# Decay exponents of a state-space layer: from a TensorE product to a broadcast load and sums on GpSimd

## What is computed

```python
xBC  = causal_depthwise_conv(W_in @ layernorm(u))       # four taps
cum  = cumsum(-softplus(A_log), within the chunk)
diff = cum[..., :, None] - cum[..., None, :]            # (q, k)
decay = exp(where(k <= q, diff, -inf))
y_intra = einsum('bchqk,bckhp->bcqhp', (C @ B^T) * decay, x)
states  = einsum('bckhn,bckhp->bchpn', B * exp(cum[-1] - cum), x)
y_inter = einsum('bcqhn,bchpn->bcqhp', C * exp(cum), previous state)
out = (y + D * x) * silu(z + z_bias) @ W_out
```

## Time and profile before

| | |
|---|---|
| median of 3 runs (lowest, highest) | 406.16 us (405.43, 406.35) |
| the profiled execution: its time, its span | 406.83 us, 405.1 us |
| TensorE busy | 386.7 us (95%) |
| VectorE busy | 332.6 us (82%) |
| ScalarE busy | 226.6 us (56%) |
| GpSimd busy | 176.2 us (43%) |
| moved by DMA | 21.13 MB, mean 52 GB/s |
| share of the chain of waits: TensorE, VectorE, ScalarE, GpSimd | 70%, 13%, 8%, 2% |

### The profile page before, as it was taken

The page is one execution under the profiler, slowest core; times in us unless marked ns, Lnnn a source line. Parts: engine busy times, 40 slices in busy tenths (PEclk is TensorE's granted clock), DMA queues, the critical chain, the costliest instruction groups (busy, mean ns, idle before and its releaser), DMA issues.

```text
span 405.1 us, 8904 instructions
## 1 busy us (share of the span) xinstructions
PE 386.7 (95%) x3023; PEld 299.3 (74%) x3023; DVE 332.6 (82%) x564; ACT 226.6 (56%) x422; POOL 176.2 (43%) x208
## 2 busy tenths in 40 slices
PE   8998999999999999996989999899999999999996
PEld 8686676766766767764767777568888888888886
DVE  5988899999999999997989938738958759696685
ACT  6766556465565564568676632664554545546541
POOL 3699411101111101106456920235686665867661
PEclk9999999999999999999999999989999999999999
DMA  6311220322220122213411150000102020200003
GB/s 186 100 54 25 58 64 8 115 56 61 62 59 28 41 59 63 61 35 109 128 49 25 49 162 1 0 2 1 60 19 78 3 78 13 65 0 2 0 2 104
DMA packets 35932, 21.13 MB, mean 52 GB/s; under 512 B 17048, under 2 KB 33760, under 8 KB 35904
## 3 DMA queue, kind: packets, MB, share of 16 engines
q1 hardware_dynamic: 35904, 20.78, 18.3%
HBM read 18.13 MB, written 1.31 MB: 48 GB/s over the span
## 4 chain that ended last, share of the span: by engine, by line
PE 70%; DVE 13%; ACT 8%; issue 6%; POOL 2%; ACTq 0%; DVEq 0%; POOLq 0%
PE bank L1283 22%; PE bank L1259 10%; PE bank L1249 9%; PE bank L1478 8%; PE bank L1252 5%; PE bank L1398 3%; PE bank L1269 2%; PE bank L1466 2%; DVE conv L1228 2%; PE bank L1307 2%; PE bank L1425 2%; DVE conv L1021 2%; POOL el L656 1%; ACT conv L695 1%; PE bank L1486 1%
## 5 line engine op out<-in xcount | busy, mean ns | idle before, releaser
L1021 DVE SCALAR_TENSOR_TENSOR conv<-bank,taps,conv 128x510 f32<-128x510 f32 (+2 forms) x204 | 149.8, 745 | 17.4 <-ACT conv L695 12.3
L1283 PE MATMUL bank<-uth,parts 128*128 128x512 f32 x272 | 95.3, 407 | 1.1 <-DVE utl L1004 0.9
L695 ACT ACTIVATE conv<-bank,tap_b,taps 128x512 f32<-128x512 f32 x68 | 52.9, 777 | 69.6 <-PE bank L1283 58.9
L569 POOL TENSOR_TENSOR ce<-conv,ecx 128x512 f32<-128x512 f32 x15 | 19.4, 1291 | 117.5 <-DVE conv L1021 117.5
L1283 PEld LDWEIGHTS bank<-uth,parts 128*128 128x128 f32 x272 | 51.0, 187 | 18.9 <-issue 3.5
L651 POOL TENSOR_TENSOR ul<-conv,uh 128x512 fp32r<-128x512 f32 x32 | 42.9, 1357 | 40.5 <-ACT uh L922 27.5
L656 POOL TENSOR_TENSOR el<-conv,parts 128x512 fp32r<-128x512 f32 x30 | 44.3, 1504 | 30.3 <-ACT parts L934 30.3
L1283 PE MATMUL bank<-utl,parts 128*128 128x512 f32 x136 | 53.5, 393 | 0.0
L1216 DVE CAST uh<-conv 128x512 fp32r<-128x512 f32 x28 | 26.0, 966 | 22.5 <-ACT conv L918 21.9
L1228 DVE TENSOR_TENSOR conv<-conv 128x512 f32<-128x512 f32 x32 | 31.4, 1014 | 11.9 <-ACT conv L939 11.8
L1106 DVE SCALAR_TENSOR_TENSOR g<-dec,bank 128x512 f32<-128x512 f32 x64 | 40.8, 678 | 0.0
(11 more groups left out here) (208 smaller groups left out, 743.3 us busy)
## 6 DMA issues: line engine op xcount, KB each, us to landing
w_raw<-in_L_attn_W_in_dram SPq DMA_DIRECT2D x17, 256.0 KB, 3.2
ecx<-ecum_dram SPq DMA_DIRECT2D x32, 128.0 KB, 2.9
ew_raw<-in_L_ffn_Wup_dram SPq DMA_DIRECT2D x7, 256.0 KB, 2.9
ew_raw<-in_L_ffn_Wgate_dram SPq DMA_DIRECT2D x7, 256.0 KB, 3.1
ew_raw<-in_L_ffn_Wdown_dram SPq DMA_DIRECT2D x7, 256.0 KB, 3.8
xres<-in_x_dram SPq DMA_DIRECT2D x2, 512.0 KB, 4.2
out_dram<-xres SPq DMA_DIRECT2D x4, 256.0 KB, 2.1
yi<-yev SPq DMA_DIRECT2D x56, 16.0 KB, 1.8
```

The costliest lines, as they stand in the source:

```text
L695: act.activation(conv[q][:, j, HALF * h:HALF * (h + 1)], bank[u % 2][:], ACT.Identity, bias=tap_b[q][:, j:j + 1], scale=taps[q][:, j, TAPS ...
L1021: dve.scalar_tensor_tensor(out=dst[:, :, d:SEQ], in0=src[:, :, 0:SEQ - d], scalar=taps[q][:, j, TAPS - 1 - d:TAPS - d], in1=dst[:, :, d:SE ...
L1283: ins = pe.matmul(bank[u % 2][:], w, x_t, start=(i == 0), stop=(i == 3 * KD - 1))
```

## The change

The exponents are no longer a matmul. `load_cumb` brings, for each unit, the four rows of cumulative sums broadcast to all 128 partitions (256 KB) into its own tile `cumb[u]`; GpSimd overwrites what the mask excludes with -1e30 (`mask`, an affine select in place) and adds the negative sum of each key (`spans`), and ScalarE takes the exponential of that tile into one of four `dec`. The masks and adds of units 0 and 1 are made a body ahead, those of 2 and 3 in the pair's own body. Each load waits for the exponential of the same unit of the pair before. `turn_w` takes the place of exponents 0 and 1; the state is turned into bank 4. The taps of two units are interleaved (`crossed_taps`), and what waits for them counts by `taps_by`. The extra work of ScalarE and GpSimd is moved to earlier bodies, and the unrolled part begins at pair 8.

```diff
-            def load_cum(m, q):
...
+            def load_cumb(m, u):
+
+                h, j = u // 2, u % 2
+                at_least(sp, exp_done, 4 * (m - 2) + u + 1)
+                row = T * (2 * (m - 1) + j) + T // 2 * h
+                sp.dma_start(cumb[u][:], cum_dram[row:row + T // 2, :].partition_broadcast(P)).then_inc(cumb_in[u], 16)
...
+        def taps_by(m, u):
+
+            in_turn = isinstance(m, int) and m < 2
+            return 12 * m + ((3, 6, 9, 12) if in_turn else (4, 6, 10, 12))[u]
...
-            for n in range(PAIRS - 4, PAIRS + 1):
+            for n in range(PAIRS - 8, PAIRS + 1):
...
-                if n == PAIRS - 3:
+                if n == PAIRS - 5:
                     load_expert(0, 0)
-                if n == PAIRS - 2:
+                if n == PAIRS - 4:
                     load_expert(1, 1)
...
                 if n < PAIRS:
-                    load_cum(n + 1, 1 - q)
+                    load_cumb(n + 1, 0)
+                    load_cumb(n + 1, 1)
                 if 1 < n < PAIRS:
                     sp.wait_ge(y_read, n - 1)
                     place_y(n - 1, 1 - q, yev_out[1 - q])
                 if n < PAIRS:
                     load_ecx(n + 1, 1 - q)
+                    load_cumb(n + 1, 2)
                 if n + 3 <= PAIRS:
                     load_w(n + 3, 1 - q)
                 if n + 2 <= PAIRS:
                     load_taps(n + 2, q)
+                if n < PAIRS:
+                    load_cumb(n + 1, 3)
...
+            def mask(u):
+
+                pool.affine_select(out=cumb[u][:], in_=cumb[u][:], compare_op=ALU.is_ge, fill=NEG, base=0,
+                                   pattern=[[0, T // 2], [1, P]], channel_multiplier=-1).then_inc(masked, 1)
+
+            def spans(n, q, u):
+
+                pool.wait_ge(masked, 4 * (n - 1) + u + 1)
+                h, j = u // 2, u % 2
+                from_s = ncp[q][:, j, 2 * h:2 * h + 2, :].rearrange("p b c -> p (b c)").unsqueeze(2).to_broadcast([P, T // 2, P])
+                pool.tensor_tensor(cumb[u][:], cumb[u][:], from_s, ALU.add).then_inc(span_done, 1)
...
+            pool.wait_ge(ncum_done, 1)
+            copy_ncum(1, 1)
...
+            mask(0)
+            mask(1)
+            spans(1, 1, 0)
+            spans(1, 1, 1)
...
             def body(n, k, q):
                 end = isinstance(n, int) and n == PAIRS
+                pool.wait_ge(cumb_in[2], 16 * n)
+                pool.wait_ge(cumb_in[3], 16 * n)
                 if end:
+                    mask(2)
+                    mask(3)
+                    spans(n, q, 2)
+                    spans(n, q, 3)
                     decay_c_half(n, q, 0)
                     decay_c_half(n, q, 1)
...
+                    gate_late()
+                    rest_weights(1, 1, 1)
+                    rest_weights(1, 1, 2)
+                    return
+                at_least(pool, stT_done, n - 1)
+                copy_xs(n + 1, 1 - q)
+                mask(2)
+                mask(3)
+                spans(n, q, 2)
+                spans(n, q, 3)
+                at_least(pool, y_done, 4 * (n - 1))
+                copy_x(n + 1, 1 - q)
+                decay_c(n, k, q)
+                at_least(pool, exp_done, 4 * (n - 1))
+                pool.wait_ge(cumb_in[0], 16 * n + 16)
+                pool.wait_ge(cumb_in[1], 16 * n + 16)
+                copy_ncum(n + 1, 1 - q)
+                mask(0)
+                mask(1)
+                pool.wait_ge(ncp_done, n + 1)
+                spans(n + 1, 1 - q, 0)
+                spans(n + 1, 1 - q, 1)
...
+                if n == 1:
+                    weigh_context()
+                if n in (PAIRS - 7, PAIRS - 6):
...
+                if n in (PAIRS - 5, PAIRS - 4):
+                    pool.wait_ge(z_gated, 4)
+                    gate_y(0, n - PAIRS + 5)
+                if n == PAIRS - 3:
...
+                    rest_weights(0, 0, 0)
+                if n == PAIRS - 2:
+                    rest_weights(0, 0, 1)
+                    rest_weights(0, 0, 2)
+                    rest_weights(1, 1, 0)
+                if n == PAIRS - 1:
+                    gate_y(1, 0)
+                    gate_y(1, 1)
...
-            act.copy(cr[1][0][STEPS:ROWS, :, :, :], rows_wide()).then_inc(cr1_done, 1)
...
+            act.activation(ncum[:].rearrange("p c r -> p (c r)"), bank[7][:, P:3 * P], ACT.Identity, scale=-1.0).then_inc(ncum_done, 1)
...
-                act.activation(dec[b][:], bank[4 + b][:], ACT.Exp).then_inc(exp_done, 1)
+                a = 4 * (n - 1) + u
+                act.wait_ge(span_done, 4 * (n - 1) + u + 1)
+                at_least(act, g_done, a - 3)
+                act.activation(dec[u][:], cumb[u][:].rearrange("p i t -> p (i t)"), ACT.Exp).then_inc(exp_done, 1)
...
-                if isinstance(n, int) and n == PAIRS - 4:
-                    gate_of_z(u)
-                if isinstance(n, int) and n == PAIRS - 3:
-                    pairwise(u)
-                if isinstance(n, int) and n >= PAIRS - 2 and u < 3:
+                if isinstance(n, int) and n in (PAIRS - 8, PAIRS - 7) and u % 2:
+                    gate_of_z(2 * (n - PAIRS + 8) + u // 2)
+                if isinstance(n, int) and n in (PAIRS - 6, PAIRS - 5) and u % 2:
+                    pairwise(2 * (n - PAIRS + 6) + u // 2)
+                if isinstance(n, int) and n in (PAIRS - 3, PAIRS - 2) and u < 3:
...
+            def crossed_taps(m, q, v):
+
+                done = 12 * m + 3 * v
+                for i, (u, d) in enumerate(((v, 1), (v, 2), (v + 1, 1), (v, 3), (v + 1, 2), (v + 1, 3))):
...
+                    if d == 1:
+                        dve.wait_ge(acc_first, 4 * m + u + 1)
+                    else:
+                        dve.wait_ge(tap_done, done + (0, 1, 0, 2, 3, 5)[i])
...
-                        other_taps(n, q, 3)
+                        if isinstance(n, int) and n == 1:
+                            other_taps(n, q, 3)
...
-                        other_taps(n + 1, 1 - q, 0)
-                        other_taps(n + 1, 1 - q, 1)
+                        crossed_taps(n + 1, 1 - q, 0)
...
-                        other_taps(n + 1, 1 - q, 2)
+                        crossed_taps(n + 1, 1 - q, 2)
...
-                pe.wait_ge(tap_done, 12 * n + (9, 12)[h])
+                pe.wait_ge(tap_done, taps_by(n, 2 + h))
...
-                exponents(n, k, q, 2)
-                exponents(n, k, q, 3)
                 b_dot_c(n, q, 1)
...
                 turn_state(n - 1)
                 weigh(n - 1, 1 - q, 2)
-                exponents(n, k, q, 0)
-                exponents(n, k, q, 1)
+                if not last(n, 2):
+                    turn_w(n + 2, k + 1, q, lambda: None)
                 from_state(n - 1, 0)
```

More of the change, by code:

```diff
@@ L103, in decoder_layer @@
         cum = sb("cum", [P, 2 * P])
[L104 to L105 removed]
+        ncum = sb("ncum", [P, 2, P])
+        ncp = [sb(f"ncp{i}", [P, 2, NSEQ, 2]) for i in range(2)]
         ecum = sb("ecum", [P, P])
@@ L204, in decoder_layer @@
         taps_in = [sem(f"taps_in{i}") for i in range(2)]
-        cum_in = [sem(f"cum_in{i}") for i in range(2)]
+        cumb_in = [sem(f"cumb_in{u}") for u in range(4)]
         ew_in = [sem(f"ew_in{i}") for i in range(2)]
@@ L372, in _ @@
                              ecum[NH * b:NH * (b + 1), :]).then_inc(ecum_out, 16)
-            sp.wait_ge(const_done, 3)
-            sp.wait_ge(cr1_done, 2)
             sp.wait_ge(cum_out, 16 * NSEQ)
-            load_cum(1, 1)
+            for u in range(4):
+                load_cumb(1, u)
             sp.wait_ge(ecum_out, 16 * NSEQ)
@@ L612, in body @@
+                mask(0)
[3 more added lines that the diff above has]
+                spans(n + 1, 1 - q, 1)
+                if not isinstance(n, int):
+                    return
+                if n == 1:
+                    weigh_context()
+                if n in (PAIRS - 7, PAIRS - 6):
+                    for v in range(2 * (n - PAIRS + 7), 2 * (n - PAIRS + 7) + 2):
                         pool.wait_ge(zgate_done, v + 1)
@@ L621, in body @@
-                    if isinstance(n, int) and n == PAIRS - 2 and u == 3:
-                        for j in range(3):
-                            rest_weights(0, 0, j)
-                    if isinstance(n, int) and n == PAIRS - 1 and u == 2:
-                        rest_weights(1, 1, 0)
-                        rest_weights(1, 1, 1)
-                        gate_y(1, 0)
-                        gate_y(1, 1)
-                        rest_weights(1, 1, 2)
-                    if u == 1 and end:
-                        gate_late()
@@ L870, in body @@
                 copy_state_turned(n)
+                if not first:
+                    act.wait_ge(ce_done, n - 1)
                 beside(n, m, km, r, 2)
@@ L1279, in project_pass @@
                         pe.wait_ge(utl_done, 2 * u + 2)
-                    at_least(pe, tap_done, 3 * (4 * m + u - 1))
+                    if u >= 2:
```

(3 more changed lines are left out.)

169 lines of the change are left out of this document (50 added, 119 removed).

## The result

The changed kernel takes 415.59 us, median of 4 runs (415.15 to 417.32), the kernel before 406.19 beside it (405.43 to 406.35): a ratio of 1.0226, 95% interval 1.0183 to 1.027. The forecast, 409.8, had the direction and not the size, and 415.59 lies above the range. The profiled execution took 415.15 with a span of 413.2.

A forecast was written before the change was run, and what follows sets the result against it. TensorE was taken to bound a pair at 12.47 us, VectorE right behind. Start +1.6, bodies 3 to 7 -1.6, bodies 8 to 15 -1.1, end +4.2 and clock +0.5 gave +3.6: 409.8 us, range 401.5 to 414.5.

The forecast's parts named there:

- the forecast loop: Plain pair: fourth tap 2.83, signal 0.1, b_dot_c to the next block's first tap 3.70, block 4.2, two g 1.30: 12.13 us.
- start: Before S(3): GpSimd's masks and adds, exponentials and split_w delay the first crossed block; +1.6 us, bounds 0.8 to 2.5.
- bodies 8 to 12: ScalarE's table load, gates of z and sigmoids, moved to these bodies, hold back copies; 4.4 us over plain pairs.
- the end's mechanism: Last pair: late loads and GpSimd's queue delay ce, so TensorE's state product starts 4.2 us later; lower bound 1.2.
- Loads: Plain pairs: 256 KB loads land after 3.2 us, worst 5.1; slack 1.8, so landing may take 5; no stall.
- rival 4: GpSimd bounds, masks at 1.29: near 421 us, chance 0.04; aside, loads landing after 5.5 us: 412 to 415, chance 0.04.
- at most about 0.4 us a pair: Plain pairs: most that removing TensorE work alone can bring, as VectorE has 12.07 us of work and 0.42 idle.
- at no cost there: Plain pairs: turn_w moves into TensorE's wait for ScalarE's copy of the state, priced at nothing.
- split_router: Bodies 8 to 15: 2.28 us of VectorE work loses its cover; less 0.56 idle, +1.7 us.
- the clock: Last pair: TensorE idles near 4 us and part of the work runs at 1.2 GHz; +0.5 us, within 0 to 1.5.
- Rival 3: Crossing the taps gives nothing: pairs take 12.47 instead of 12.13 in some nine bodies, 412.9 us; chance 0.12.
- Rival 1: VectorE becomes the bound at 11.57 us a pair and the end is cheap: 402.4 us; chance 0.33 for the group.

The follow-up runs named there:

- the last run: Kernel before, exponents still on TensorE, with only the first block of taps of each pair crossed: 405.65 us, ratio 0.9982.
- the six traces of the table: Changed kernel and five edits of it (taps in turn, router spread, sig loads moved, end reordered, transfer from ScalarE), all keeping 1024 single values: body 4 stalls 2.6 to 6.8 us.
- the second candidate: Changed kernel with 32-byte runs reordered by GpSimd, end reordered, split_w(3) and table load moved, router in last pair, only first tap block crossed: 397.08 us, ratio 0.9763.
- ScalarE's queue: Changed kernel with the transfer of 1024 single values issued by ScalarE behind body 2 instead of by SyncE: 418.04 us, ratio 1.0294.
- the run with the end's two moves: Changed kernel with late loads spread behind those of cumb, and GpSimd making the first half of ce before the second gate of y: 409.59 us, ratio 1.0083.

## Why the prediction was right or wrong

**Right: the bound before, the loop after.** TensorE set the pair with VectorE just behind, as the last run shows from the other side. A plain pair was forecast at 12.13 and took 12.06, the block 4.18, and the chain is the forecast loop. The Trainium skill's "The DRAIN you can't avoid" ("VectorE: DVE Perf Modes") would have left the block at 4.45; it took 4.18, so the row was the better guide here too.

**Right, near: start, bodies 8 to 12, the end's mechanism.** The start cost 1.6, forecast 1.6, though S(3) moved by 0.9 between kernels with the same start. Bodies 8 to 12 took 65.12; the forecast had 5 x 12.13 + 4.4 = 65.05, and each of the five bodies came within 0.1 of its term. The state product came at S(16)+13.0, forecast 13.5, for the reasons given, late loads and GpSimd's order; moving both together took it away.

**Wrong: "Loads". The step that failed** is "A 256 KB load lands after 3.2 us, worst 5.1... Plain pairs hold." The worst case was taken from transfers with nothing unusual ahead of them. Behind the 1024 single values loads landed after 10.3 us, against a slack of 1.8 by the prediction's own count, and the weight tile after 6.85. Bodies 3 to 7 came out 3.6 us over their term, 4.1 of it in body 4. The prediction counted how many transfers SyncE issues and their bytes, but not that one of them was of another kind. It held the effect only as an aside of rival 4 (landings after 5.5 us, 412 to 415, chance 0.04); that aside is the nearest to what happened, in one body and at 415.59. Before, the same transfer was issued at 57.6, landed after 7.3, and from 57 to 75 no engine waited for a transfer.

**Wrong: "at most about 0.4 us a pair" for removing TensorE work alone.** It was taken from 12.07 us of VectorE work. With the taps in turn the pair is 11.86, all of it VectorE's work: from the first of two g to what follows it is 1.19 us, not 1.27 and 1.30. So the gain of a plain pair, 0.4, does not come from the crossing, without which the prediction had left the pair at 12.47: crossing both blocks took 0.2 back from the 0.6 of the other edits. The loop that was forecast for the crossed pair was right; what the pair costs without crossing was not.

**Wrong: turn_w "at no cost there".** The price was right as a price, the four products do fit into the wait for the state, but the move is more than free: it is worth 0.5 us a pair (12.16 against 11.63), since the slot had been the first exponents', while the removal without the move is worth 0.3. In body 4 it turned round: turn_w now stands ahead of the state products and b_dot_c, and the late weight tile held all of these for 3.15 us. The price of nothing had left out that the tile must now be there earlier: in the six traces of the table the chain of body 4 runs through it. GpSimd's spans came late in the same body, off the chain; how long the body would be with them alone late, no run shows.

**Mis-sized: split_router**, 2.28 less 0.56 taken, +1.7. The piece took 3.36, as GpSimd works beside it now, and the pair was 3.5 over a plain one. That is 1.8 over its term, where bodies 8 to 15 together missed theirs by 1.6. The cover that was gone had been seen; that GpSimd's new work would sit beside it had not.

**Mis-sized: the clock**, 0.5 taken within 0 to 1.5, for the end alone. Behind the wait that ended at 244.98 the granted clock fell (0.58 from 246 to 248, 0.56 from 248 to 250), and the projection took 1.65 and 1.71 per four products instead of 1.03; the mean of the stretch was 0.91. S(16) to the statistics grew by 5.4, of which the late state product explains 3.7 (13.0 less 9.3); 1.7 came behind it. In body 4 the clock was priced at nothing; the table puts some 1.5 of its 4.1 us there (4.1 less 2.6), an estimate. The -1.5 behind the statistics was not forecast, and no run was made on it: before, the clock stood at 0.70 from 260 to 265; after, the table of stretches shows 1.00 throughout 252 to 330.

**GpSimd's prices** erred on the safe side in sum: mask 0.64 (forecast 0.60), add 1.05 (forecast 1.29), 8.3 us a pair (25.02 for three) against 9.7.

**The rivals.** Rival 3 asked whether crossing shortens the pair and set the base at 12.47. The question was right and the base wrong: without it the pair is 11.86. Rival 1, VectorE as the bound at 11.57 a pair, is what the second candidate reaches (11.63), with one block crossed and not two.

## What to carry to other kernels

List the kinds of transfers, not only their number and bytes: one with single-value runs delayed the loads issued behind it, from either queue tried, and a change that narrows the slack of loads makes it visible. When work of one engine is removed and the next engine's order is changed with it, price each with and without the other: here, one step on the other, crossing the first block brings nothing (12.45), the removal 0.3 (12.17), the move of turn_w for which it makes room 0.5 (11.63), and crossing the second block takes back 0.4 (12.06). Ask of what is moved earlier when its own input arrives. And give a new wait of TensorE more than its own length: the wait of 3.15 us in body 4 made it 4.1 longer, that of 2.58 at the end went with 5.4.

## What the runs showed of the hardware

- Single values: 1024 in one transfer delayed loads of cumb behind it to 9.9 to 13.2 us in six traces (median of all 3.5 to 3.6), and the weight tile to 6.8 to 9.6; two transfers of 128 held GpSimd as well (10.5 us from the loads' issue to its start, though the worst landing that the view of that run gives is 7.4); the same bytes in runs of 32 did not (worst 5.5). With ScalarE's queue, the trace has no packet on any engine from 65 to 67, behind the values. The stall ranged from 2.6 to 6.8 us, 2.6 and 2.7 where the granted clock stayed at 1.00. What holds the loads, and why the later ones of the eight transfers stalled nothing, stays open.
- VectorE's casts beside GpSimd: the 72x256 cast took 0.35 us beside one of GpSimd's gates of y (in the run with the end's two moves), 0.61 and 0.73 beside its selects and adds, and 3.12 in the last pair of the second candidate, from 225.89 to 229.01, through a select's end, two adds, and products back to back. The taps, kept 0.66 and 0.77 all along. The Trainium skill, "GPSIMD Engine Reference", section "Key points", says that GpSimd shares its SBUF interfaces with VectorE and contends with its two-port modes and two-input instructions. That fits the subtraction of two SBUF tiles (0.55 to 0.96); whether a cast runs in such a mode, no trace here shows. That one cast spanned several GpSimd instructions in a row (3.12) is what the trace shows.
- A GpSimd sum whose second operand is broadcast along the row took 1.05 us at 128x512, one of two full operands 1.29.
